# Graph experts and routed gated experts of the last layer in one block, the norm between them tile by tile, the gates in column groups

## The chip, the cores and the metric

The kernel runs on one core of one Trainium2 chip. Its engines are TensorE (PE, with its weight loads as PEld), VectorE (DVE), ScalarE (ACT), GpSimd (POOL) and SyncE (SP), each with its own queue of instructions; they wait for one another through semaphores. The metric is device time in microseconds (us), the median of several runs.

## What is computed

Four layers, each a graph layer and a feed-forward layer, on 512 tokens of 512 numbers. The change touches the feed-forward layer of layer 0 (only its gate) and both halves of layer 3:

```
# layer 3, graph half: 4 experts of two convolutions, the best 2 per token
gates = softmax(x @ gate_W + gate_b);  top_v, top_i = top_k(gates, 2)
sage_conv(h) = (sum of h over incoming edges / degree) @ W_l + b_l + h @ W_r
for e in 4 experts: h = x; for l in 2: h = relu(sage_conv(h))
out = sum over the chosen two of h_e * top_v
# layer 3, feed-forward half: 8 gated experts, the best 2 per token
logits = flat @ router_w.T;  topk_w = softmax(top_k(logits, 2))
y = (silu(flat @ w_gate) * (flat @ w_up)) @ w_down,   summed with topk_w
# around both
x = x + graph(_layernorm(x));   x = x + ffn(_layernorm(x))
```

Layer 0's feed-forward half routes each token to the best of 8 experts.

## The kernel before

Tokens are held as T = 4 tiles of P = 128 rows: `k.X` is the running sum, `k.N` its normed rows, `k.NT` the same turned (features on the partitions). PSUM has 8 banks, `k.ps[:, b, :]`. The program is written engine by engine; within an engine the written order is the order of work, and there is no scheduler. A `nc.Block()` holds one stage for all engines, and ends when all have ended it.

- **Gate** (`Routing`). `products` multiplies the gate's weights (8 or 4 columns) with `NT`, four matmuls that accumulate in 8 or 4 partitions (L829). ACT copies the result to SBUF (L892), `turns` (L836) turns it to rows of tokens, and `vector` (from L854 or L857) picks the experts. It is used in layer 0's feed-forward half and twice in layer 3.
- **Norm** (`Norm`). DVE makes statistics of all four tiles (L519, L522), ACT one root (L546), DVE the rows (L526), PE 16 transposes (L557), ACT and DVE two copies each (L549, L540). Ahead of its first wait PE runs 9 matmuls on zeros (`keep_busy`, L292).
- **Routed experts** (`RoutedFfn`). After the gate PE counts ranks (L1053, L1056) from the chosen experts' marks. DVE works out each token's place in a list sorted by expert, in granules of 128. The first granule is gathered by PE with a one-hot matrix (`place`, L1178; L1065), all others go by way of memory: POOL scatters all rows to `spread_d` (L1311, 8 indirect transfers of 128 rows in layer 3, 4 in layer 0), and when all have landed SP loads the second granule's tokens (L1023) and weights. PE then multiplies granule by granule: first weights (L1088), turn of the next granule's tokens (L1070), second weights (L1107). SP issues, ahead of all this, the gate's weights (L821), zeros for `spread_d` (L961) and the first granule's weights (L972, L977).
- **Graph experts** (`sage`). For each of 4 experts PE runs: own and neighbour products of layer 1 (L2888, L2920), two products of layer 2 for all four tiles (L2931, then L2936), and then the neighbour sums for all four tiles (L2943), which need the first product cut into a high and a low part (`hi`, `lo`: L2994, L2995; semaphore `ready`). DVE adds tile by tile into X (L2999, L3003 to L3007). Experts 0 and 1 are written out, 2 and 3 run in a loop. Weights lie in two sets `W[0]`, `W[1]`; SP loads expert e's when expert e - 2 has ended (`heads`).

Layer 3's graph half is one block, its feed-forward half the next; the second starts with `Norm`.

## Time and profile before

| what | value |
|---|---|
| time, median of 3 runs | 2035.28 us (2035.04 to 2037.95) |
| the profiled execution, whole / span of the trace | 2033.54 / 2031.8 us |
| PE busy | 1898.8 us, 93% |
| DVE / ACT / POOL busy | 952.7 / 499.7 / 318.8 us |
| mean TensorE clock granted | 0.974 of full speed |
| stages that the change touches | layer 0 gate 318 to 334, graph experts 1508 to 1781, last norm, gate and experts 1781 to 2032 us |

All times within the trace count from the span's start. A row of the timeline gives start, duration, engine, line, operation, what is written and read, shape, count, and in brackets how long the engine was idle before and who ended that. An f32 matmul is recorded as two instructions, a transpose as one. Busy time of PE says little by itself, since matmuls overlap; the distance between the starts of rows says what they cost.

### The profile page before, as it was taken

What the parts mean: (1) busy time and instruction counts of PE and PEld (TensorE: products, weight loads), DVE (VectorE), ACT (ScalarE), POOL (GpSimd) and SP (SyncE); (2) the same over time, 40 slices, a digit from 0 to 9 for tenths busy, and PEclk for the clock granted to TensorE, in tenths of its full rate; (3) what the DMA queues carried; (4) which work ended last, traced back from release to release, by engine and by line L of the source; (5) the groups of instructions that cost most, each with busy time, mean ns of one, the idle gap of its engine ahead of it and who ended that gap; (6) DMA issues with size and microseconds to landing.
All of it is one profiled execution on the core that took longest, in us unless ns stands there. A gap on an engine that the chain in (4) does not pass through costs nothing. (4 is left out here: it accounts for less than half of the span.)

```text
span 2031.8 us, 27351 instructions
## 1 busy us (share of the span) xinstructions
PE 1898.8 (93%) x8967; PEld 1042.6 (51%) x8967; DVE 952.7 (47%) x2888; ACT 499.7 (25%) x1379; POOL 318.8 (16%) x342
## 2 busy tenths in 40 slices
PE   8998997999989999999999799879789999979999
PEld 4454455766735434543453333334434444458876
DVE  7464455100069886998698721156432223240102
ACT  0153352111134361225224412137110000010000
POOL 0000000333407502740471000000000000010001
PEclk9999998999989999999999899989899999989999
DMA  4003008998358603740578199943352220089884
GB/s 165 1 1 104 1 2 333 399 358 328 118 170 268 179 1 129 238 119 1 150 214 284 41 329 386 386 144 127 124 180 80 88 88 0 0 311 403 326 316 157
DMA packets 180666, 358.02 MB, mean 176 GB/s; under 512 B 28816, under 2 KB 38304, under 8 KB 180524
## 3 DMA queue, kind: packets, MB, share of 16 engines
q1 hardware_dynamic: 157548, 285.94, 38.9%
q0 software_dynamic: 22976, 70.23, 11.6%
q8 instruction: 84, 1.38, 0.3%
q14 instruction: 58, 0.48, 0.1%
HBM read 334.43 MB, written 21.69 MB: 175 GB/s over the span
## 5 line engine op out<-in xcount | busy, mean ns | idle before, releaser
L1088 PEld LDWEIGHTS ps<-tokT,w 128*128 128x128 f32 x2304 | 259.8, 192 | 10.7 <-issue 6.7
L1088 PE MATMUL ps<-tokT,w 128*128 128x128 f32 x2304 | 260.6, 275 | 3.1 <-DVE tokT L1233 3.1
L1546 POOL DMA_INDIRECT w<-xl_d,src_i x216 | 213.3, 987 | 293.3 <-DMA xl_d<-XL 225.2
L1642 PE MATMUL ps<-XP,wide 128*128 (+1 forms) x456 | 185.2, 507 | 0.0
L1647 PE MATMUL ps<-w,ident 128*128 128x512 f32 x270 | 140.3, 601 | 8.2 <-DMA w<-xl_d,src_i 7.9
L1642 PEld LDWEIGHTS ps<-XP,wide 128*128 128x128 f32 x456 | 81.6, 189 | 72.6 <-issue 67.3
L1757 ACT ACTIVATE wide<-oht 128x128 fp32r<-128x128 bf16 x228 | 68.1, 308 | 196.9 <-PE ps L1647 176.9
L1311 POOL DMA_INDIRECT spread_d<-N,slot x12 | 11.8, 980 | 664.3 <-DVE slot L1192 661.2
L1107 PE MATMUL ps<-w,O 128*128 128x512 f32 x256 | 111.2, 592 | 0.0
L1919 DVE SCALAR_TENSOR_TENSOR w<-ps,w 128x512 f32<-128x512 f32 x144 | 98.1, 682 | 4.1 <-PE ps L1647 3.7
L1247 DVE TENSOR_TENSOR hT<-act,ps 128x512 f32<-128x512 f32 x20 | 13.8, 688 | 178.5 <-ACT act L1140 178.5
L1942 DVE SCALAR_TENSOR_TENSOR M<-pen,L,M 128x128 bf16 (+1 forms) x228 | 78.8, 346 | 9.9 <-DVE L L1931 6.1
L1148 ACT ACTIVATE O<-ps,b 128x128 f32<-128x128 f32 x128 | 36.5, 368 | 188.4 <-PE ps L1088 188.4
L1107 PEld LDWEIGHTS ps<-w,O 128*128 128x128 f32 x256 | 48.0, 190 | 57.4 <-issue 57.4
L261 POOL DMA_INDIRECT edges_d<-payload,slots x68 | 65.3, 960 | 49.2 <-ACT O L1148 35.7
L1689 PE MATMUL ps<-w 128*128 128x512 f16 x304 | 69.8, 380 | 1.6 <-DVE w L2002 1.0
L1107 PE MATMUL ps<-w,hT 128*128 128x512 f32 x160 | 70.3, 592 | 0.0
L392 PE MATMUL ps<-oh_d,oh_s 128*128 128x512 bf16 x272 | 67.3, 383 | 2.3 <-DVE oh_d L363 2.3
L292 PE MATMUL ps<-zero 128*128 128x512 bf16 x167 | 47.3, 439 | 22.4 <-PEq L2050 9.0
L2994 DVE CAST hi<-ps 128x512 fp32r<-128x512 f32 x16 | 11.1, 692 | 121.2 <-PE ps L2931 121.2
L2814 POOL DMA_INDIRECT tok<-rows_d,at_c x4 | 4.0, 1001 | 384.2 <-DVE at_c L2762 383.3
L1647 PEld LDWEIGHTS ps<-w,ident 128*128 128x128 f32 x270 | 48.4, 188 | 27.6 <-DMA w<-xl_d,src_i 18.2
(518 smaller groups left out, 3051.4 us busy)
## 6 DMA issues: line engine op xcount, KB each, us to landing
w<-L_ffn_W SPq DMA_DIRECT2D x16, 2048.0 KB, 12.8
w<-L_ffn_W SPq DMA_DIRECT2D x8, 4096.0 KB, 17.6
w<-fc1T SPq DMA_DIRECT2D x32, 1024.0 KB, 14.2
w<-fc2T SPq DMA_DIRECT2D x30, 1024.0 KB, 14.2
w<-L_ffn_w_gate SPq DMA_DIRECT2D x20, 1024.0 KB, 9.2
w<-L_ffn_w_up SPq DMA_DIRECT2D x20, 1024.0 KB, 12.1
w<-L_ffn_w_down SPq DMA_DIRECT2D x10, 2048.0 KB, 15.2
w<-L_ffn_w SPq DMA_DIRECT2D x8, 2048.0 KB, 13.2
```

The costliest lines, as they stand in the source:

```text
L261: gp.indirect_dma_start(k.edges_d, bass.IndirectOffsetOnAxis(ap=self.slot[:, j:j + 1].bitcast(U32), axis=0), self.pay[:, j, :], None).then ...
L292: m = pe.matmul(k.ps[:, b, :], k.zero16[:, 0:P], k.zero16[:], start=True, stop=True)
L392: pe.matmul(k.ps[:, T + t, :], oh_s[u][:, t * P:(t + 1) * P], oh_d[u][:], start=(i == 0), stop=(i == ET - 1))
L1088: m = pe.matmul(k.ps[:, 1 + (q * ins + i) % 4, s * P:(s + 1) * P], self.W1[u][i][:, f, (q * T + s) * P:(q * T + s + 1) * P], self.tokT[:, ...
L1107: m = pe.matmul(k.ps[:, 5 + u, :], self.hT[:, s, :], self.W2[u][:, s, :], start=(s == 0), stop=(s == self.HT - 1))
L1546: gp.indirect_dma_start(self.G[:, u, :], None, k.xl_d, bass.IndirectOffsetOnAxis(ap=k.src_i[:, i:i + 1].bitcast(U32), axis=0)).then_inc(k. ...
L1642: m = pe.matmul(bank, self.wide[:, i % DEEP, :], self.XP[:, q].rearrange("p t n -> p (t n)")[:, bass.ds(at, D)], start=False, stop=(q == 1 ...
L1647: m = pe.matmul(bank, k.ident[:], self.source(i), start=False, stop=True)
L1689: m = pe.matmul(k.ps[:, T:2 * T, :].rearrange("p b n -> p (b n)")[:, bass.ds(at, N)], half[u], self.os[l][u], start=False, stop=True, skip ...
L1757: a.activation(self.wide[:, i % DEEP, :], self.oht[:, i * P:(i + 1) * P], ACT.Copy).then_inc(self.widened.sem, 1)
L1919: v.scalar_tensor_tensor(self.r[i % QUAD], rows, 0.0, self.att8, ALU.max, ALU.mult, accum_out=self.sdot[:, i:i + 1]).then_inc(self.dotted. ...
L1942: v.scalar_tensor_tensor(low, self.pen[:, i * P:(i + 1) * P], self.L[:, i:i + 1], low, ALU.subtract, ALU.min).then_inc(self.low.sem, 1)
```

## The change

1. `Routing.products` writes each of its four matmuls to a group of 32 output partitions of its own (weights padded with zeros to 32 columns, `pad`, on POOL) and doesn't accumulate. `turns` becomes four matmuls with `k.pile`, a matrix that adds the four groups up while it turns them; `k.pile` is made once by one DVE reduction at the start of the program.
2. `RoutedFfn.tensor` gets 9 matmuls on zeros ahead of the ranks and 7 behind them, in both routed layers.
3. `sage` and the last `RoutedFfn` are one block. The experts' loop is written out. The experts' weights, some temporaries and the gate's rows lie in the routed layer's buffers: `W[0]` in its first granule's first weights.
4. SP issues the router's weights, the zeros and the first granule's second weights behind the last graph expert's weights, and the first granule's first weights as soon as graph expert 2 has ended.
5. PE runs L2936's product and the neighbour sum of a tile one after the other, for every expert, and DVE follows.
6. In the last expert the norm is made tile by tile (`TileNorm`), between the experts' tiles; the router's logits are made as rows of tokens (`row_logits`, moving side 8 columns), so that no turn is needed. 12 matmuls on zeros stand ahead of the last tile's transposes.

```diff
@@ Routing @@
     def products(self, pe, bank=0):
...
         for f in range(T):
-            m = pe.matmul(k.ps[0:width, bank, :], self.g[:, f, :], self.cols[:, f, :], start=(f == 0), stop=(f == T - 1))
+            m = pe.matmul(k.ps[f * GATE:(f + 1) * GATE, bank, :], self.g[:, f, :], self.cols[:, f, :],
+                          start=True, stop=True)
...
     def turns(self, pe, bank=0):
...
         for t in range(T):
-            m = pe.transpose(k.ps[:, bank, t * 8:t * 8 + width], self.logits_at[0:width, t * P:(t + 1) * P],
-                             k.ident[0:width, 0:width])
+            m = pe.matmul(k.ps[:, bank, t * 8:t * 8 + width], self.logits_at[:, t * P:(t + 1) * P],
+                          k.pile[:, 0:width], start=True, stop=True)
...
+    def row_logits(self, pe, t, bank):
...
+        for f in range(T):
+            m = pe.matmul(k.ps[:, bank, t * 8:t * 8 + width], self.cols[:, f, t * P:(t + 1) * P],
+                          self.g[:, f, 0:width], start=(f == 0), stop=(f == T - 1))
...
+class TileNorm:
...
+    def statistics(self, v, ch, t):
+        ch.link(v.bn_stats(self.st[:, t, :], self.x[:, t, :]))
+        v.bn_aggr(self.mv[:, t, :], self.st[:, t, :]).then_inc(self.stats.sem, 1)
+
+    def roots(self, a, t):
+        a.wait_ge(self.stats.sem, self.stats.at(t + 1))
+        a.activation(self.rstd[:, t:t + 1], self.mv[:, t, 1:2], ACT.Sqrt, bias=self.k.eps[:, 0:1]
+                     ).then_inc(self.root.sem, 1)
+
+    def normal(self, v, ch, t):
+        v.wait_ge(self.root.sem, self.root.at(t + 1))
+        ch.link(v.reciprocal(self.rstd[:, t:t + 1], self.rstd[:, t:t + 1]))
+        v.tensor_scalar(self.rows[:, t, :], self.x[:, t, :], self.mv[:, t, 0:1], self.rstd[:, t:t + 1],
+                        ALU.subtract, ALU.mult).then_inc(self.normed.sem, 1)
+
+    def turn(self, pe, t, bank):
+        pe.wait_ge(self.normed.sem, self.normed.at(t + 1))
+        for f in range(T):
+            m = pe.transpose(self.k.ps[:, bank, f * P:(f + 1) * P], self.rows[:, t, f * P:(f + 1) * P],
+                             self.k.ident[:])
+        m.then_inc(self.turned.sem, 1)
...
@@ RoutedFfn.tensor @@
+        keep_busy(pe, k, 3, 9)
         pe.wait_ge(k.chosen.sem, k.chosen.at(1))
...
         i.then_inc(k.ranks.sem, 1)
+        keep_busy(pe, k, 3, 7)
...
@@ sage, SP @@
                 for e in range(2, E):
                     sp.wait_ge(k.heads.sem, k.heads.at(e - 1))
                     weights(sp, e, e % 2)
+                ffn.r.sync(sp)
+                ffn.empty(sp)
+                ffn.second_weights(sp, 0, 0)
+                sp.wait_ge(k.heads.sem, k.heads.at(E - 1))
+                ffn.first_weights(sp, 0, 0)
+                ffn.sync(sp)
...
@@ sage, PE @@
                         m.then_inc(k.av.sem, 1)
-                    pe.wait_ge(k.ready.sem, k.ready.at(1) + e)
-                    for t in range(T):
+                        if e == E - 1 and t >= 2:
+                            closing.wait_columns(pe, t - 2)
+                            ffn.r.row_logits(pe, t - 2, 0)
+                        if t == 0:
+                            pe.wait_ge(k.ready.sem, k.ready.at(1 + e))
                         for part in (hi, lo):
...
                         m.then_inc(k.out.sem, 1)
-                walk(pe, step)
+                        if e == E - 1 and t:
+                            closing.turn(pe, t - 1, t - 1)
+                for e in range(E):
+                    step(e)
+                closing.wait_columns(pe, T - 2)
+                ffn.r.row_logits(pe, T - 2, 0)
+                keep_busy(pe, k, 5, 12)
+                closing.turn(pe, T - 1, T - 1)
+                closing.wait_columns(pe, T - 1)
+                ffn.r.row_logits(pe, T - 1, 0)
+                ffn.tensor(pe)
...
@@ sage, DVE, last expert @@
                         m = v.tensor_tensor(k.X[:, t, :], k.X[:, t, :], o[:, t, :], ALU.add)
-                    m.then_inc(k.heads.sem, 1)
-                    v.wait_ge(k.heads.sem, k.heads.at(1) + e)
+                        if e == E - 1:
+                            ch.link(m)
+                            closing.statistics(v, ch, t)
+                            closing.normal(v, ch, t)
```

PE's queue from the last graph expert's products of layer 2 to the last layer's ranks, before (in the loop's body, so the rows stand for experts 2 and 3):

```order
L2936 MATMUL ps<-w,H_347 128x512 x16
L2943 MATMUL ps<-hi,C 128x512 x4
L2943 MATMUL ps<-lo,C 128x512 x4
...
L2943 MATMUL ps<-hi,C 128x512 x4
L2943 MATMUL ps<-lo,C 128x512 x4
...
L292 MATMUL ps<-zero_20 128x512 x9
L557 MATMUL ps<-ident,N 128x128 x16
L829 MATMUL ps<-NT,gate 8x512 x4
L836 MATMUL ps<-ident,tok 128x8 x4
L1053 MATMUL ps<-m,beforeb 128x8
```

The same place after, from the last expert's third tile on (L3030 is the product that was L2936, L3040 the neighbour sum, L959 the transposes, L907 the gate rows, L293 the matmuls on zeros, L1130 the ranks):

```order
L3030 MATMUL ps<-w_358,H_396 128x512 x4
L907 MATMUL ps<-gate,NT 128x8 x4
...
L959 MATMUL ps<-ident,N 128x128 x4
L3030 MATMUL ps<-w_358,H_396 128x512 x4
L907 MATMUL ps<-gate,NT 128x8 x4
...
L959 MATMUL ps<-ident,N 128x128 x4
L907 MATMUL ps<-gate,NT 128x8 x4
L293 MATMUL ps<-zero_20 128x512 x12
L959 MATMUL ps<-ident,N 128x128 x4
L907 MATMUL ps<-gate,NT 128x8 x4
L293 MATMUL ps<-zero_20 128x512 x9
L1130 MATMUL ps<-m,beforeb 128x8
```

What moved: products, sums, transposes and gate rows of different tiles now alternate (where "..." stands after, the sum of that tile is left out, two rows of L3040), and only one tile's transposes and gate rows are left behind the last sum.

SP's queue at the same place, before (the last rows of the graph block, then the next block):

```order
L2849 DMA b_362<-sage_b 128x512
L2861 UNCONDITIONAL_BRANCH
...
L821 DMA gate<-router_wT 128x4x8
L961 DMA spread_d<-zrow 128x512 x14
L972 DMA w_381<-L_ffn_w_gate 128x4x512
L972 DMA w_382<-L_ffn_w_up 128x4x512
...
L977 DMA w_385<-L_ffn_w_down 128x8x512
```

And after:

```order
L2937 DMA b_403<-sage_b 128x512
L827 DMA gate<-router_wT 128x4x8
L1038 DMA spread_d<-zrow 128x512 x14
L1052 DMA w_359<-L_ffn_w_down 128x8x512
L1047 DMA w_355<-L_ffn_w_gate 128x4x512 [waits heads]
L1047 DMA w_356<-L_ffn_w_up 128x4x512
```

What moved: no block border stands between the graph weights and the routed layer's, the second weights come ahead of the first, and the first wait for graph expert 2 alone.

## Rows read from the trace of the kernel before

**Rows 1.** The page, first part: busy us, share of the span, instructions.

```profile
PE 1898.8 (93%) x8967; PEld 1042.6 (51%) x8967; DVE 952.7 (47%) x2888; ACT 499.7 (25%) x1379; POOL 318.8 (16%) x342
```

**Rows 2.** Timeline, last graph expert, PE and DVE.

```profile
1757.43 13.90 PE L2936 MATMUL ps<-w,H 128*128 128x512 f32 x32
...
1758.36 0.69 DVE L2995 TENSOR_TENSOR lo<-ps,hi 128x512 fp32r<-128x512 f32 x1
...
1773.04 1.09 PE L2943 MATMUL ps<-hi,C 128*128 128x512 f32 x4
1773.30 0.75 DVE L3003 SCALAR_TENSOR_TENSOR o<-ps,inv_deg,o 128x512 f32<-128x512 f32 x1 [1.24 <-PE ps L2943]
...
1774.90 1.09 PE L2943 MATMUL ps<-hi,C 128*128 128x512 f32 x4
...
1780.35 0.69 DVE L3007 TENSOR_TENSOR X<-X,o 128x512 f32<-128x512 f32 x1
```

**Rows 3.** Timeline, from the last norm to the second granule.

```profile
1781.57 3.72 PE L292 MATMUL ps<-zero 128*128 128x512 bf16 x9 [2.78 <-PEq L2861]
1781.57 2.47 DVE L519 BATCH_NORM_STATS2 stats<-X 128x6 f32<-128x512 f32 x4 [0.53 <-PEq L2861]
...
1784.49 0.30 ACT L546 ACTIVATE rstd<-mv,eps 128x4 f32<-128x4 f32 x1 [1.67 <-DVE mv L522]
...
1785.63 2.03 PE L557 MATMUL ps<-ident,N 128*128 128x128 f32 x16 [0.34 <-DVE N L526]
1787.37 1.08 ACT L549 ACTIVATE NT<-ps 128x512 f32<-128x512 f32 x2 [2.58 <-PE ps L557]
...
1788.83 3.60 PE L829 MATMUL ps<-NT,gate 128*8 128x512 f32 x8 [1.16 <-DVE NT L540]
...
1793.55 0.19 DVE L857 COPY lg<-ps 128x32 f32<-128x32 f32 x1 [4.78 <-PE ps L836]
...
1795.65 0.19 PE L1053 MATMUL ps<-m,beforeb 128*128 128x8 bf16 x1 [2.14 <-DVE m L1168]
...
1797.68 6.06 PE L1065 MATMUL ps<-w,N 128*128 128x128 f32 x32 [1.49 <-DVE w L1178]
...
1804.53 14.56 PE L1088 MATMUL ps<-tokT,w 128*128 128x128 f32 x128 [0.78 <-DVE tokT L1233]
...
1820.16 0.66 PE L1070 MATMUL ps<-ident,tok 128*128 128x128 f32 x4 [1.08 <-DMA tok<-spread_d]
```

**Rows 4.** The same timeline, last scatter on POOL, then SP.

```profile
1809.22 0.96 POOL L1311 DMA_INDIRECT spread_d<-N,slot  x1 [0.30 <-issue]
...
1817.67 0.34 SPq L1023 DMA_DIRECT2D tok<-spread_d  x1
```

**Rows 5.** Timeline, gate of layer 0, PE alone.

```profile
322.39 0.41 PE L836 MATMUL ps<-ident,tok 8*128 8x8 f32 x4 [0.68 <-ACT tok L892]
326.33 0.19 PE L1053 MATMUL ps<-m,beforeb 128*128 128x8 bf16 x1 [3.54 <-DVE m L1166]
...
328.11 5.31 PE L1065 MATMUL ps<-w,N 128*128 128x128 f32 x32 [1.24 <-DVE w L1178]
334.21 1.05 PE L1088 MATMUL ps<-tokT,w 128*128 128x128 f32 x7 [0.79 <-DVE tokT L1233]
```

**Rows 6.** Stretches: length, busy us by engine, granted clock, DMA share, GB/s.

```profile
325.00:330.00 5.00, 2.42 (x23) 2.34 (x24) 3.93 (x27) 0.17 (x1) 0.00 (x0) 0.50 1.04 388
...
1796.00:1802.00 6.00, 4.51 (x28) 4.42 (x25) 4.25 (x24) 1.21 (x1) 1.38 (x2) 0.50 1.05 409
```

**Rows 7.** Groups by form, PE: busy us, mean ns of one, idle before.

```profile
L2690 PE MATMUL ps<-w,hT 128*32 128x512 f32 x64 | 7.7, 598 | 3.2 <-ACT hT L2806 3.2
...
L2706 PE MATMUL ps<-g,NT 128*128 128x16 f32 x32 | 4.8, 298 | 1.2 <-PEq L449 1.2
```

**Rows 8.** DMA issues of two stretches: count, median us from issue to landing.

```profile
spread_d<-N,slot POOLq DMA_INDIRECT x8, 6.5
...
NT<-result_d,back_slot POOLq DMA_INDIRECT x4, 3.5
```

More of the change, by code:

```diff
@@ L50 @@
 EX_SCALE = 16384.0
+GATE = P // T
 class Ticker:
@@ new lines, with __init__, columns, wait_columns @@
+class TileNorm:
+    def __init__(self, k, c, x, rows, cols):
+        self.k, self.x, self.rows, self.cols = k, x, rows, cols
+        self.stats, self.root, self.normed, self.turned, self.cols_out = signals(
+            c, k, "tile_stats", "tile_root", "tile_rows", "tile_turned", "tile_columns")
+        self.st, self.mv, self.rstd = sb(c, k, "stats", [P, T, 6]), sb(c, k, "mv", [P, T, 2]), sb(c, k, "rstd", [P, T])
+    def statistics(self, v, ch, t):
[16 more added lines that the diff above has]
+        m.then_inc(self.turned.sem, 1)
+    def columns(self, a, t, bank):
+        a.wait_ge(self.turned.sem, self.turned.at(t + 1))
+        a.activation(self.cols[:, :, t * P:(t + 1) * P],
+                     self.k.ps[:, bank, :].rearrange("p (f n) -> p f n", f=T), ACT.Copy).then_inc(self.cols_out.sem, 1)
+    def wait_columns(self, eng, t):
+        eng.wait_ge(self.cols_out.sem, self.cols_out.at(t + 1))
@@ L899, in done, with __init__ @@
     def done(self):
-        k = self.k
-        done((k.gate_loaded, 32 if self.bias is not None else 16), (k.gate_mm, 1), (k.gate_rows, 1), (k.gate_turned, 1), (k.gate_ready, 1), (k.gate_exped, 1))
+        done((self.stats, T), (self.root, T), (self.normed, T), (self.turned, T), (self.cols_out, T))
 class RoutedFfn:
-    def __init__(self, k, c, r, norm, granules, w, hidden, gated, spread, result, beside=None, spare=None, y=None):
+    def __init__(self, k, c, r, norm, granules, w, hidden, gated, spread, result, beside=None, spare=None, y=None,
+                 joined=False):
@@ L912, in __init__ @@
         self.k, self.r, self.norm, self.granules, self.w, self.gated, self.beside = k, r, norm, granules, w, gated, beside
-        self.rows, self.out = norm.rows, y
+        self.rows, self.out, self.joined = norm.rows, y, joined
         self.summed, self.last_placed, self.last_turned, self.last_cols, self.last_added = signals(
@@ L1046, in tensor @@
         n_first, n_second, n_third = self.counts()
-        self.norm.tensor(pe)
-        self.norm.wait_cols(pe)
-        self.r.tensor(pe)
+        if not self.joined:
+            self.norm.tensor(pe)
+            self.norm.wait_cols(pe)
+            self.r.tensor(pe)
+        keep_busy(pe, k, 3, 9)
         pe.wait_ge(k.chosen.sem, k.chosen.at(1))
@@ L1126, in scalar @@
         k, quads, ins = self.k, self.quads, self.ins
-        self.norm.scalar(a)
-        self.r.scalar(a)
+        if self.joined:
+            self.r.exps(a)
+        else:
+            self.norm.scalar(a)
+            self.r.scalar(a)
         signal = k.ffn_act if self.gated else k.ffn_hidden
@@ L1223, in vector @@
         k, quads = self.k, self.quads
-        self.norm.vector(v)
+        if not self.joined:
+            self.norm.vector(v)
         self.r.vector(v, chosen=self.choose)
@@ L1306, in pool @@
         k, choices, G = self.k, self.r.choices, self.granules
+        if not self.joined:
+            self.r.pad(gp)
         gp.wait_ge(k.emptied.sem, k.emptied.at(16 * (G - 1)))
@@ L2861, in sage @@
         with nc.Block() as block:
-            def walk(eng, step):
-                for u in range(2):
-                    step(u, u, 0)
-                with eng.Fori(1, E // 2) as j:
-                    for u in range(2):
-                        step(j * 2 + u, u, j)
             @block.sync
@@ L2902, in means, with step @@
                         m.then_inc(neighbors.sem, 1)
-                def step(e, u, j):
-                    if not later(e, 1):
+                def step(e):
+                    u = e % 2
+                    if e == 0:
                         pe.wait_ge(rooted.sem, rooted.at(16))
```

153 lines of the change are left out of this document (95 added, 58 removed).

## The prediction, before the changed kernel ran

> **What bounds the kernel now.** I read the page first: TensorE (PE) is busy for 93% of the span [rows 1], so whatever shortens the time must either take work off PE or close one of its pauses. The chain that ended last does not reach back far enough to help, so I went through the timeline of the three places that the diff touches, and asked at each who waits last.
>
> The last expert of the graph layer [rows 2] is a PE stretch without pause: the fourth product of each tile (L2936) for all four tiles, 13.90 us, that is 3.43 a tile, and then the neighbour sums (L2943), 1.87 us a tile (1773.04 to 1774.90). VectorE (DVE) follows them at 1.9 us a tile and ends its last addition to X at 1781.04. Then [rows 3] comes a chain in which every engine works on all four tiles and hands them on whole: statistics 1781.57, root 1784.49, transposes 1785.63, gate product 1788.83, routing from 1793.55, ranks 1795.65, the first granule's gather 1797.68, and only at 1804.53 the first expert product. From the end of PE's last neighbour sum (1773.04 + 3 x 1.87 = 1778.64) to there it is 25.9 us, in which PE does little that counts. The first product of the second granule waits again, 1.08 us, for rows that were scattered to memory and read back: the scatters were issued from 1800.32 to 1809.22 and the row tile asked for at 1817.67 [rows 4]. After that PE has no pause worth naming, so what is gained up to there is kept. The gate of the first routed layer has the same shape [rows 5]: turn 322.39, ranks 326.33 after 3.54 us of pause, gather 328.11.
>
> TensorE's granted clock was 0.50 in both stretches in which ranks and gather stand [rows 6], the lower of its two levels (1.2 GHz); before each, PE had been mostly idle while DVE chose experts.
>
> **The change, part by part.**
>
> Gate in column groups (first routed layer and graph layer). Four matmuls of 8 or 4 output partitions that accumulated now go to four groups of 32 output partitions. Before: 3.60 us for 8 recorded instructions (two for each f32 matmul) [rows 3, 7]. Nearest row: L2690, also 32 partitions by 512 elements in four groups, 64 in 7.7 us, so 0.12 each and about 1.0 for the 8. Saved: 2.6. From both sides: nothing, if the groups didn't run together (3.6), and 2.7. L2690 has the very shape, so I take 2.6. The turn becomes four f32 matmuls with a full 128x128 stationary side: 8 instructions. L2706 with 16 columns took 0.15 each, partly at the lower clock [rows 7], L1088 0.114 each at the higher one (14.56 over 128) [rows 3]. I take 0.12, 1.0 in all against 0.41, so 0.6 lost (bounds 0.5 and 0.8). Net 2.0 in each layer. In the graph layer nothing else waits there: weights and inverse degrees are there early. The Trainium skill ("TensorE: Matmul & The Clock Gate", Part 3, measured speedup) gives 2.38 times for three column tiles; by that rule four would give, as an estimate, about 3 and save 2.4 instead of 2.6, where this trace shows 3.6 (0.43 over 0.12).
>
> Fill matmuls in both routed layers: 9 ahead of the ranks, 7 behind them. Nine of them took 3.72 at the lower clock [rows 3], so about 1.9 at the higher and 1.5 for seven. The pause ahead of the ranks is 3.54 in the first layer [rows 5] and 2.14 in the last [rows 3]: the nine are covered at the higher clock, and not at the lower (3.7). The seven fill a pause of 1.24 [rows 5] and 1.49 [rows 3]: 0.3 and 0.1 lost. What they give: if the clock stays up, the gather of 32 instructions costs 32 x 0.114 plus a tail, 3.8, in place of 5.31 and 6.06: 1.5 and 2.3 gained. First layer in sum: -2.0 + 0.3 - 1.5 = **-3.2**. Its first weights were there when the tokens' copy was (PE went on 0.79 after it [rows 5]); the queue is full until past 330 [rows 6], so if they had landed only then, up to 3.2 would go: the low bound of this term is 0. Graph layer: **-2.0**.
>
> Loops written out, output sums between products (all experts). PE now does product and sum tile by tile; the same instructions in another order, so 0 as long as the first sum finds its high and low parts ready. They are ready at 1759.05 (1758.36 and 0.69) and would be wanted at 1757.43 + 3.43 = 1760.86 [rows 2]: 1.8 us in hand. Weights for the last routed layer's first granule and the zeros move ahead into the last two experts, where the queue has nothing to carry.
>
> Last norm tile by tile. PE does four more things before the last tile's sum ends: transposes of tiles 0 and 1 (2.03 / 4 = 0.5 each [rows 3]) and their gate rows (8 x 0.12 = 0.95 each): +2.9, so 1778.64 becomes 1781.5, and X of tile 3, 2.25 later as now (0.26, then 1.99), 1783.75. From there, for one tile, by [rows 3]: statistics 2.47 / 4 = 0.62, from their end to the root at most 0.45 (1784.04 to 1784.49), the root 0.30, from its end to the first transpose 0.84 (1784.79 to 1785.63): 2.2, so the rows are there at 1786.0. PE meanwhile: transposes of tile 2 (0.5), its copy (0.2 and 0.54), its gate rows (0.95), then 12 fill matmuls (12 x 0.21 = 2.6): free at 1786.4. The fill is the last to end, by 0.4. Then transposes 0.7 with tail, copy 0.65, gate rows 1.1: DVE reads the logits at 1788.9, against 1793.55: **-4.65**. The new exponential's table load falls into the routing, as now. With gather (-2.3) and fill (+0.1) the first expert product starts 6.85 earlier, at 1797.7, and ends at 1812.25.
>
> Second granule. Its rows hang on the scatter, which only moves by 4.65: last issue 1804.57. The issue costs the same on GpSimd (POOL). But before, weights kept the DMA engines full (share 1.05 [rows 6]): a scatter took 6.5 us to land, an indirect transfer with a quiet queue 3.5 [rows 8]. After, the weights are there already. From the last issue to SP's request it was 8.45 [rows 4]; with 3.5 in place of 6.5 it is 5.45 (bounds 3.5 and 8.45): asked for at 1810.0, there 2.5 after that (1817.67 to 1820.16 now): 1812.5. PE comes at 1812.25 and waits 0.25. Last layer in sum, by the second granule's start: 1812.5 - 1820.16 = **-7.7**.
>
> Constants: one small reduction on DVE at the start, +0.2 (0 if hidden).
>
> Sum: -3.2 - 2.0 - 7.7 + 0.2 = -12.7. The profiled execution took 2033.54, the median of the three runs is 2035.28, so I set the change against the median: **2022.6 us**.
>
> **Rivals.**
> 1. Clock. In the first layer the turn would end at 320.8 (322.39 - 2.6 + 1.0), the nine at 322.7, and the ranks start at 324.3 (326.33 - 2.0): PE still idles for 1.6 us. If the clock falls there as it does now, seven fillers cost 2.9 for a pause of 1.24 (+1.65) and the gather stays at 5.3: the layer gives 0.35 instead of 3.2, total 2025.4. For it: rows of 0.50 after pauses; against: the pause is less than half of the old one. Chance 0.20.
> 2. The same in the last layer: nine fillers 3.7 against a cover of 2.1 (+1.7), seven +1.5, gather 6.8 (+3.0). The layer gives 1.7 instead of 7.7 (1820.16 against 1812.25 + 6.2), total 2028.6, and 2031.4 with rival 1 as well. The Trainium skill has a rule for this ("TensorE: Matmul & The Clock Gate", Part 4): transposes don't count as activity for the clock. Against it, between the transposes stand 12 + 9 + 7 real matmuls and no pause above 0.9. Chance alone 0.05, both 0.05.
> 3. The scatter lands no sooner with a quiet queue. Then 1804.57 + 8.45 + 2.5 = 1815.5, PE waits 3.2, total 2025.6. Against it speaks [rows 8]. Chance 0.08.
> 4. Slower: PE now meets the wait for high and low parts after one tile's product and not after four. Were DVE late by x beyond the 1.8 in hand, each of four experts would cost x. To end slower than before by 0.2% it takes 17 us, 4.2 an expert, so DVE ready 6 us later than in [rows 2]. DVE is idle for over 2 us between its pairs of casts. Chance 0.03.
> 5. The column groups don't overlap: 5.2 lost, total 2027.8. Chance 0.04.
>
> **How the numbers follow.** All works as summed: 0.50, between 2018.5 and 2024.5 (copy and handoff times, the 12 fillers, drift of the clock elsewhere). With rivals 1 to 5 at 0.45 and 0.05 for what I don't see. 2018 to 2029 leaves out both clocks low, the slower case and half of the unseen on either side, 0.12 or so. A measurement of this kernel can tell about 0.2%, 4 us, from no change. Faster by more than that: 0.50 + 0.20 + 0.05 + 0.08 + 0.04 and some of the unseen, 0.89; within 0.2%: both clocks low and some of the unseen, 0.07; slower: 0.04.
>
> **What the profile of the changed kernel would show.** The gate product at about 1.0 us; granted clock 1.00 from the ranks through the gather in both layers and a gather under 4 us; DVE's logits copy some 7.4 us after the last neighbour sum's end; W1 of the last layer 16 us after it and not 25.9; scatters that land in under 4 us and no PE pause before the second granule; PE without pauses in the four experts. A PE pause ahead of the first neighbour sum, or a clock of 0.50 at the gather, or more than 1 us waiting for the scattered rows, would make it wrong.

## The result, and the profile after

The changed kernel took 2017.3 us (median of 4 runs, 2016.1 to 2019.47) against 2035.16 us for the kernel before (4 runs beside it, 2032.65 to 2037.95). The ratio is 0.9913, with a 95% interval of 0.9896 to 0.993, so it is faster, by 0.9%. The forecast was 2022.6 in a range from 2018 to 2029: the sign and most of the mechanism hold (in layer 0 the clock did not do what was forecast), and the time lies 0.7 us below the range.

The page of the kernel after, first part (busy us, share of the span, instructions), answers to [rows 1]. PE is busy for 4.1 us less, although 44 matmuls on zeros were added (the nine of the last norm, L292, are gone), and the span is 14.2 us shorter: the other 10.1 us are pauses that are closed or filled, and PE's share of the span goes from 93% to 94%.

```profile
span 2017.6 us, 27480 instructions
PE 1894.7 (94%) x9030; PEld 1044.4 (52%) x9030; DVE 953.2 (47%) x2890; ACT 500.6 (25%) x1383; POOL 318.9 (16%) x344
```

**The last layer.** Timeline of the kernel after, from the last expert to the second granule (start, length, engine, line, operation, count, idle before and what ended it). It answers to [rows 2 to 4].

```profile
1751.86 3.60 PE L3030 MATMUL ps<-w,H 128*128 128x512 f32 x8
...
1775.71 0.60 PE L959 MATMUL ps<-ident,N 128*128 128x128 f32 x4
...
1776.99 1.06 PE L907 MATMUL ps<-gate,NT 128*128 128x8 f32 x8 [0.69 <-ACT NT L965]
...
1777.91 2.75 PE L293 MATMUL ps<-zero 128*128 128x512 bf16 x12
...
1779.48 0.55 DVE L953 TENSOR_SCALAR N<-X,mv,rstd 128x512 f32<-128x512 f32 x1
...
1780.49 0.60 PE L959 MATMUL ps<-ident,N 128*128 128x128 f32 x4
...
1781.78 1.06 PE L907 MATMUL ps<-gate,NT 128*128 128x8 f32 x8 [0.69 <-ACT NT L965]
...
1782.69 2.10 PE L293 MATMUL ps<-zero 128*128 128x512 bf16 x9
1782.88 0.19 DVE L869 COPY lg<-ps 128x32 f32<-128x32 f32 x1 [2.85 <-PE ps L907]
...
1784.98 0.18 PE L1130 MATMUL ps<-m,beforeb 128*128 128x8 bf16 x1 [0.19 <-DVE m L1249]
...
1787.01 3.84 PE L1143 MATMUL ps<-w,N 128*128 128x128 f32 x32
...
1791.63 14.56 PE L1166 MATMUL ps<-tokT,w 128*128 128x128 f32 x128 [0.78 <-DVE tokT L1315]
...
1798.58 0.96 POOL L1395 DMA_INDIRECT spread_d<-N,slot  x1 [0.30 <-issue]
...
1802.13 0.34 SPq L1098 DMA_DIRECT2D tok<-spread_d  x1
...
1806.03 0.60 PE L1148 MATMUL ps<-ident,tok 128*128 128x128 f32 x4
```

Count everything from the last expert's fourth product (L3030; L2936 in [rows 2]). To the logits copy it is now 31.02 us (1782.88 - 1751.86), before 36.12 (1793.55 - 1757.43): -5.10. From the copy to the ranks (2.10) and on to the gather (2.03) nothing has changed, so the fill matmuls cost nothing there. From the gather to the first expert product 4.62 in place of 6.85: -2.23. From there to the second granule 14.40 in place of 15.63: -1.23, most of it the pause of 1.08 for the scattered rows, which is gone. In all -8.56.

Its stretches (length, busy us by engine, granted clock, DMA share, GB/s), which answer to the second row of [rows 6]:

```profile
1516.00:1700.00 184.00, 184.00 (x487) 91.43 (x486) 50.12 (x100) 10.26 (x16) 0.00 (x0) 1.00 0.31 111
1700.00:1800.00 100.00, 97.66 (x391) 56.45 (x389) 36.49 (x95) 10.97 (x17) 7.75 (x8) 1.00 0.17 61
1800.00:2017.00 217.00, 212.07 (x1416) 170.65 (x1414) 31.51 (x57) 17.32 (x29) 12.66 (x17) 1.00 0.82 300
```

The granted clock stays at its higher level (2.4 GHz) through the ranks and the gather. The DMA issues from 1785 to 1805 (count, KB each, median us to landing), beside [rows 8]:

```profile
tok<-spread_d SPq DMA_DIRECT2D x1, 256.0 KB, 2.6
spread_d<-N,slot POOLq DMA_INDIRECT x8, 2.9
```

**The gate of layer 0.** The same kernel's timeline, PE alone, beside [rows 5]:

```profile
320.20 1.93 PE L840 MATMUL ps<-NT,gate 128*32 128x512 f32 x8 [0.95 <-DVE NT L543]
322.85 1.88 PE L848 MATMUL ps<-pile,tok 128*128 128x8 f32 x8 [0.72 <-ACT tok L915]
324.58 3.60 PE L293 MATMUL ps<-zero 128*128 128x512 bf16 x9
328.13 0.18 PE L1130 MATMUL ps<-m,beforeb 128*128 128x8 bf16 x1
...
328.49 1.67 PE L293 MATMUL ps<-zero 128*128 128x512 bf16 x7
330.00 3.73 PE L1143 MATMUL ps<-w,N 128*128 128x128 f32 x32
334.52 5.74 PE L1166 MATMUL ps<-tokT,w 128*128 128x128 f32 x49 [0.78 <-DVE tokT L1315]
```

Product, turn and the nine fill matmuls ran at the lower clock (1.2 GHz): 1.93 and 1.88 in place of the 1.0 that was forecast for each, and the nine took 3.60. The clock came back while they ran, and PE had no pause ahead of the ranks. Nor did the nine hold the ranks up. They start at 328.13, 0.06 us after DVE has made the marks that they read, as they do where PE stands waiting for these (old gate, below):

```profile
327.89 0.18 DVE L1247 CAST m<-masks 128x32 bf16<-128x32 f32 x1
```

The gather took 3.73, at the higher clock. From the gate product to the first expert product: 14.3 us.

**The gate of the graph layer**, the same view:

```profile
1513.22 1.06 PE L840 MATMUL ps<-NT,gate 128*32 128x512 f32 x8 [0.99 <-DVE NT L543]
...
1518.65 0.95 PE L848 MATMUL ps<-pile,tok 128*128 128x4 f32 x8
...
1537.31 4.88 PE L3014 MATMUL ps<-A,w 128*128 128x512 f32 x11
```

Both as forecast; from the gate product to the first product with the neighbour means (L3014) 24.09 us, 26.26 in the kernel before.

### The profile page after: what moved, and what is told of

Its sections match the earlier page's. It is cut to its first block and busy times, and to the rows that moved or that the text cites. A ratio compares the mean times of both kernels' runs of the same rounds, so it can differ in the third digit from the quotient of the medians.

```text
span 2017.6 us, 27480 instructions
## 1 busy us (share of the span) xinstructions
PE 1894.7 (94%) x9030; PEld 1044.4 (52%) x9030; DVE 953.2 (47%) x2890; ACT 500.6 (25%) x1383; POOL 318.9 (16%) x344
## 5 line engine op out<-in xcount | busy, mean ns | idle before, releaser
L293 PE MATMUL ps<-zero 128*128 128x512 bf16 x202 | 51.8, 407 | 19.9 <-PEq L2137 9.0
L2325 PE MATMUL ps<-w,xa 128*64 128x512 f32 x256 | 58.1, 597 | 3.9 <-issue 2.9
## 6 DMA issues: line engine op xcount, KB each, us to landing
w<-fc1T SPq DMA_DIRECT2D x32, 1024.0 KB, 14.2
w<-fc2T SPq DMA_DIRECT2D x30, 1024.0 KB, 14.2
w<-L_ffn_w_up SPq DMA_DIRECT2D x20, 1024.0 KB, 12.7
```

The costliest lines, as they stand in the source:

```text
L2325: m = pe.matmul(k.ps[u * SL:(u + 1) * SL, q, :], XA[:, f, e * SL:(e + 1) * SL], W1[u][:, f, q * 512:(q + 1) * 512], start=(f == 0), stop=( ...
```

## The experiments

Each kernel was timed beside the kernel before on the same chip. Chips and executions differ by more than some of the effects (the kernel before had medians from 2033.6 to 2035.4), so runs are compared by their ratio to the kernel before; 0.001 is 2.0 us. Each ratio has an interval of some 0.0012 to 0.0024 either way, 2 to 5 us. What is finer than that is read from the stretches of the profiles, which stand together in the table at the end of this section. Every kernel computes all of the output.

**The two kernels again**, unedited, for the spread.

> The changed kernel once more, against the kernel before. The trace of the changed kernel shows 12.9 us less in the three places that the change touches (first gate 2.0, graph layer's gate 2.2, last layer 8.7), while the medians differ by 17.9. Theory A (the places are all of it, the rest is drift of untouched stages from run to run): with more rounds the difference falls to 12 to 15 us, 2020 to 2023 where before is 2035, and the untouched stages move by other amounts in this profile than in the first. Theory B (something outside the three places became shorter for good): the difference stays at 16 to 20 us, and the same untouched stages are shorter by the same amounts again.

> The kernel before, unchanged, against itself: what a comparison tells from nothing. Both theories: within 1.5 us of the kernel before. In its profile, theory A expects the starts of untouched stages (the second attention, the graph attention, the positional layer) to differ from the first profile of the same kernel by 1 to 3 us, as they do between before and after; theory B expects less than 1 us.

Measured: after 2017.51 (6 runs, 2014.37 to 2021.99), ratio 0.9911 (0.9895 to 0.9928). Before 2033.58 (12 runs, 2029.39 to 2038.27), ratio to its own other runs 0.9994 (0.9982 to 1.0006). So the gain is there again: 17.9 us against the medians beside it, as theory B has it, and 16.1 against these 12 runs. But nothing outside the three places became shorter for good: what is left of the span without them was 1926.7 and 1924.0 in the kernel before, 1925.0 and 1925.7 in the kernel after, and that is theory A. Timeline of the second profile of the kernel before, layer 0, and two of its stretches:

```profile
318.36 5.61 PE L829 MATMUL ps<-NT,gate 128*8 128x512 f32 x8 [0.95 <-DVE NT L540]
...
330.34 6.57 PE L1065 MATMUL ps<-w,N 128*128 128x128 f32 x32 [1.24 <-DVE w L1178]
337.69 2.50 PE L1088 MATMUL ps<-tokT,w 128*128 128x128 f32 x20 [0.78 <-DVE tokT L1233]
```

```profile
316.00:320.00 4.00, 3.04 (x9) 1.23 (x8) 1.29 (x2) 1.08 (x2) 0.00 (x0) 0.50 1.02 414
...
332.00:336.00 4.00, 4.00 (x20) 4.00 (x20) 1.11 (x7) 0.00 (x0) 2.47 (x3) 0.50 1.05 385
```

The same code, 3.2 us longer than in [rows 5] (19.3 from gate product to first expert product against 16.1): this time the low clock lay over the gate product (5.61) and over the whole gather (6.57 against 5.31). The forecast had priced the first layer from one execution, in which the low clock fell beside the work.

**All fill matmuls taken out.**

```diff
-        keep_busy(pe, k, 3, 9)
...
-        keep_busy(pe, k, 3, 7)
...
-                keep_busy(pe, k, 5, 12)
```

> The changed kernel without its matmuls on zeros (9 and 7 in both routed layers, 12 ahead of the last tile). If they are what keeps the clock up in the last layer, ranks and gather there run at a granted 0.50 again and the gather takes about 6 us and not 3.8: slower than the changed kernel by some 2 to 3 us there; in the first layer, where nine of them ran at the lower clock, next to nothing changes for the nine, and the gather is longer by 1 to 1.5. In all 3 to 4.5 us slower than the changed kernel. Rival (the fillers only cost PE time, the clock stays up by itself since the chain got shorter): 1 us faster than the changed kernel, gather 3.8 in the last layer.

Measured: 2024.72, ratio 0.9947 (0.9929 to 0.9964), so some 7 us of the gain hang on them by the ratios, more than the 3 to 4.5 expected. Its timeline at the two gathers:

```profile
328.05 5.81 PE L1141 MATMUL ps<-w,N 128*128 128x128 f32 x32 [1.24 <-DVE w L1257]
```

```profile
1791.25 6.35 PE L1141 MATMUL ps<-w,N 128*128 128x128 f32 x32 [1.49 <-DVE w L1257]
```

Its stretches say +2.0 in layer 0 and +3.4 in the last, 5.4 together. The rival, that the clock stays up by itself, falls.

**The fill matmuls put into the kernel before** (nine ahead of the ranks, seven behind, nothing else).

```diff
         self.r.tensor(pe)
+        clear_banks(pe, k, [3] * 9)
         pe.wait_ge(k.chosen.sem, k.chosen.at(1))
...
         i.then_inc(k.ranks.sem, 1)
+        clear_banks(pe, k, [3] * 7)
```

> The kernel before with nothing but the matmuls on zeros, 9 ahead of the ranks and 7 behind them, in both routed layers. Theory C (the gate of layer 0 is longer or shorter by where the clock happens to be low, 16.1 and 19.3 us from gate product to first expert product in two profiles of before, and fillers hold it at its shortest): about 15 us there in this profile, and 1 to 4 us off the whole, 2031 to 2034. In the last layer the gather takes 3.8, but the second granule's start stays 41.7 us behind the last neighbour sum, since it hangs on the scatter. Rival D (the fillers are worth 7 us wherever they stand, as the median without them says): 2027 to 2029.

Measured: 2030.94 (12 runs), ratio 0.9991 (0.9975 to 1.0007): no gain that this can tell. In its profile both gathers are short (3.73 and 3.84), and layer 0 gains 1.5 us (14.61, about the 15 that theory C names). The last layer's expert product starts 2.2 us earlier (44.88 us after the fourth product, not 47.10), but from there to the second granule it takes 16.99 in place of 15.63, because the scattered rows are late on the full queue, and behind that pause of 2.43 the clock falls once more (+1.7). In the last layer, alone, the fill matmuls run into the next wait. Rival D (7 us wherever they stand) falls.

**Only the 12 taken out, and 6 left of the 12.**

```diff
-                keep_busy(pe, k, 5, 12)
```

```diff
-                keep_busy(pe, k, 5, 12)
+                keep_busy(pe, k, 5, 6)
```

> The kernel after without the 12 fill matmuls between the last but one tile's gate rows and the last tile's transposes; the 9 and 7 around the ranks stay. Theory A, the nine and seven alone hold the clock: the last tile's transposes start 0.4 us earlier, as its rows were ready then, and the time is 2017.1. Theory B, TensorE's idle 2.3 us there are enough for the granted clock to be 0.50 at the ranks: the nine take 3.6, the seven 2.9 and the gather 6.1 in place of 1.8, 1.7 and 3.8, and the second granule starts some 3.5 us later: 2021.

> The kernel after with 6 fill matmuls in place of the 12. Theory A, six hold the clock as well and end before the last tile's rows are ready: the second granule starts 0.4 us earlier, 2017.1. Theory B, half of them is too little and the granted clock falls to 0.50 at the ranks: 2021.

Measured: 2017.67, ratio 0.9923 (0.9903 to 0.9942), and 2017.2, 0.9918 (0.99 to 0.9937). Neither can be told from the kernel after. The timeline without the 12, and its stretches:

```profile
1777.00 1.12 PE L959 MATMUL ps<-ident,N 128*128 128x128 f32 x4 [2.03 <-DVE N L953]
1778.80 1.88 PE L907 MATMUL ps<-gate,NT 128*128 128x8 f32 x8 [0.69 <-ACT NT L965]
1780.91 3.06 PE L293 MATMUL ps<-zero 128*128 128x512 bf16 x8 [0.23 <-issue]
...
1785.67 3.73 PE L1143 MATMUL ps<-w,N 128*128 128x128 f32 x32
```

```profile
1776.00:1780.00 4.00, 2.31 (x10) 1.92 (x10) 0.71 (x2) 2.00 (x3) 0.00 (x0) 0.56 0.00 0
1780.00:1784.00 4.00, 3.77 (x20) 1.93 (x21) 2.47 (x21) 1.16 (x3) 0.00 (x0) 0.59 0.00 0
1784.00:1788.00 4.00, 4.00 (x40) 3.20 (x38) 3.21 (x18) 0.38 (x1) 0.00 (x0) 1.00 0.00 0
```

Neither theory was right. The clock did fall, as B said, beside a pause of 2.03 and PE's transposes, and the transposes and gate rows cost double. But it rose while the nine behind them ran, and the gather ran at the higher clock. The nine held the ranks up here, by 1.0 us (3.09 from the logits copy to the ranks in place of 2.10). The price by the profile is 1.6 us (six: 0.7), not 3.5.

**The gate as it was**, in both layers that have it: accumulated product and transposes.

```diff
-            m = pe.matmul(k.ps[f * GATE:(f + 1) * GATE, bank, :], self.g[:, f, :], self.cols[:, f, :],
-                          start=True, stop=True)
+            m = pe.matmul(k.ps[0:width, bank, :], self.g[:, f, 0:width], self.cols[:, f, :],
+                          start=(f == 0), stop=(f == T - 1))
...
-            m = pe.matmul(k.ps[:, bank, t * 8:t * 8 + width], self.logits_at[:, t * P:(t + 1) * P],
-                          k.pile[:, 0:width], start=True, stop=True)
+            m = pe.transpose(k.ps[:, bank, t * 8:t * 8 + width], self.logits_at[0:width, t * P:(t + 1) * P],
+                             k.ident[0:width, 0:width])
...
```

> The changed kernel with the gate's products as one accumulation in 8 or 4 partitions and the transposes, as before. Both theories: 2.2 us more from the graph layer's gate product to its first neighbour product (26.3 against 24.1). In layer 0 theory C expects 1 to 2 us more, since fillers still keep the clock up. In all 3 to 4 us slower than the changed kernel. If column groups were worth more than that in the whole, 2023 or above, they would do something outside their own place.

Measured: 2020.32, ratio 0.9932 (0.9909 to 0.9955), which alone can't be told from the kernel after. The graph layer's stretch is back at 26.27 (+2.2). Layer 0 costs only 0.3 more (14.61 against 14.31), less than the 1 to 2 expected, but these two are not alike: in this execution product and turn ran at the higher clock, in the kernel after at the lower one. In two of the kernels below that keep the new gate (weights late, order of sums) they ran at the higher clock too, and the stretch is 12.7 there. Like with like, the column groups give 1.9 in layer 0.

**The last norm on all four tiles**, behind the last expert (the tile-wise statistics, roots, copies, transposes and gate rows out of the last expert, and the 12 with them).

```diff
-                        if e == E - 1 and t >= 2:
-                            closing.wait_columns(pe, t - 2)
-                            ffn.r.row_logits(pe, t - 2, 0)
...
-        ffn = RoutedFfn(k, c, r3, TileNorm(k, c, k.X, k.N, k.NT), G3,
+        ffn = RoutedFfn(k, c, r3, Norm(k, c, k.X, k.N, k.NT), G3,
...
```

> The changed kernel with the last norm on all four tiles after the last expert, and the gate by products and turn, as in the other layers; joined block, weights ahead, column groups and the 9 and 7 fillers stay. The sum from rows: logits some 2 us earlier than before (column groups), gather 3.8 and not 6.1, scatter onto an empty queue, and PE spared the 2.6 us of transposes and gate rows between its sums. Second granule 36.3 us behind the last neighbour sum, where the changed kernel has 30.6 and its last sum 2.6 later: 3 us slower than the changed kernel, about 2020.5. If tile by tile is most of the gain (5 us or more), the sum misses something in the norm.

Measured: 2020.51, ratio 0.9936 (0.9912 to 0.996), which alone can't be told from the kernel after either. From the last expert's fourth product to the second granule 59.24 us, 5.1 more than in the kernel after. Timeline, PE:

```profile
1778.68 3.67 PE L560 MATMUL ps<-ident,N 128*128 128x128 f32 x16 [0.83 <-DVE N L529]
...
1786.25 3.53 PE L293 MATMUL ps<-zero 128*128 128x512 bf16 x9
...
1791.48 3.73 PE L1143 MATMUL ps<-w,N 128*128 128x128 f32 x32
```

The clock fell again: the transposes of the whole norm (3.67 in place of the 2.03 of [rows 3]) and most of the nine (3.53) ran at the lower one. From the first transpose to the gate product it is 4.63 us, 3.20 in the kernel before, and from the logits copy to the ranks 3.18 in place of 2.10, since the nine end late. Those are 2.5 us; what is left of the 5.1 is near the 3 us that were expected for the chain of four tiles.

**Weights and zeros late**: the last routed layer's first weights and the zeros are issued only behind the last tile's statistics.

```diff
                 ffn.r.sync(sp)
-                ffn.empty(sp)
-                ffn.second_weights(sp, 0, 0)
                 sp.wait_ge(k.heads.sem, k.heads.at(E - 1))
+                sp.wait_ge(closing.stats.sem, closing.stats.at(T))
+                ffn.empty(sp)
                 ffn.first_weights(sp, 0, 0)
+                ffn.second_weights(sp, 0, 0)
```

> The changed kernel with zeros, first and second weights of the first granule issued only when the last tile's statistics are there, as late as before relative to the norm. If the weights have to be ahead for the shorter chain to count: PE waits for the first weights until about 1798, 6.5 us after the tokens are turned, and the scatter waits for the zeros: 5 to 7 us slower than the changed kernel, 2023 to 2025. Rival (PE would not have waited, the weights' place is worth only the scatter's landing): 0 to 2 us slower.

Measured: 2025.3 (12 runs), ratio 0.9959 (0.9944 to 0.9974). Timeline, PE, and its DMA issues:

```profile
1793.09 9.73 PE L1166 MATMUL ps<-tokT,w 128*128 128x128 f32 x64 [6.87 <-DMA w<-L_ffn_w_up]
1803.82 7.41 PE L1166 MATMUL ps<-tokT,w 128*128 128x128 f32 x64 [1.01 <-DMA w<-L_ffn_w_up]
```

```profile
w<-L_ffn_w_up SPq DMA_DIRECT2D x2, 1024.0 KB, 13.9
...
spread_d<-N,slot POOLq DMA_INDIRECT x8, 7.0
```

The second granule starts 9.7 us later, more than the 5 to 7 expected: 6.1 of them are there at the first expert product, and 3.6 come behind it, since its first 64 instructions ran partly at the lower clock behind the long pause (9.73, against 7.41 for the next 64) and PE waited once more (1.01). A faster chain needs its weights sooner, so moving them ahead is not free cover: without it the other parts lose more than half of their gain. The scatters took 7.0 beside these loads; here that cost nothing, since PE came later still.

**The queue kept full while the scatters run**: three more loads of 1 MB into dead tiles, their data unused, and the second weights behind them.

```diff
-                ffn.second_weights(sp, 0, 0)
                 sp.wait_ge(k.heads.sem, k.heads.at(E - 1))
                 ffn.first_weights(sp, 0, 0)
+                sp.wait_ge(k.chosen.sem, k.chosen.at(1))
+                for n, m in enumerate((A0, H1, o)):
+                    sp.dma_start(m[:], ...).then_inc(k.loaded.sem, 16)
+                ffn.second_weights(sp, 0, 0)
                 ffn.sync(sp)
+                sp.wait_ge(k.loaded.sem, k.loaded.at(48))
```

> The changed kernel with the first granule's second weights (2 MB) and 3 MB of loads that nobody reads issued when the experts are chosen, so that the DMA queues are full while the tokens are scattered, as they were before. If the full queue made the scatter slow: landing 6 to 7 us after each issue instead of 2.7 to 3.8, SP asks for the tokens some 3 us later, PE waits 1.5 to 3 us ahead of the second granule, and the kernel is 1.5 to 3 us slower than the changed one. Rival (the scatter's landing has its own length): no pause, and the same time.

Measured: 2017.73 (4 runs, 2015.91 to 2024.43), ratio 0.9911 (0.9893 to 0.9929): not to be told from the kernel after. Its profile (of the execution that took 2024.43) shows the mechanism, in the DMA issues, the timeline and one stretch:

```profile
spread_d<-N,slot POOLq DMA_INDIRECT x8, 7.0
```

```profile
1809.30 0.66 PE L1148 MATMUL ps<-ident,tok 128*128 128x128 f32 x4 [2.54 <-DMA tok<-spread_d]
1809.79 8.73 PE L1185 MATMUL ps<-w,hT 128*128 128x512 f32 x16
```

```profile
1812.00:1816.00 4.00, 4.00 (x9) 1.82 (x8) 0.50 (x1) 0.00 (x0) 0.00 (x0) 0.82 1.05 396
```

A scatter took 7.0 us to land in place of 2.9, and PE waited 2.54. Behind the pause the clock fell, and the sixteen products took 8.73 in place of 7.03 (in the kernel before they took 7.03 behind a pause of 1.08). The stretches say +2.7 to the second granule and +1.7 behind it. The median doesn't show these 4.4 us, and the record doesn't say why: the other three runs took 2015.91 to 2018.58, and only the slowest of the four was profiled. So the mechanism is shown in one execution, and its price in the time is not.

**The order of sums and products**: experts 0 to 2 with all products first, as before.

```diff
+                        if e < E - 1:
+                            continue
...
+                    if e < E - 1:
+                        pe.wait_ge(k.ready.sem, k.ready.at(1 + e))
+                        for t in range(T):
+                            for part in (hi, lo):
...
```

> The kernel after with the neighbour sums of experts 0 to 2 behind all four products of the expert, as before; the last expert is as after. Theory A, the order is worth nothing: from the first neighbour product to the last expert's fourth product 214.6 us as in both kernels, 2017.5. Theory B, a part of the gain that the stretches of single profiles don't show comes from this order (DVE's and ScalarE's work beside it is spread otherwise): 2019 to 2020.

Measured: 2018.11, ratio 0.993 (0.9907 to 0.9952), no difference that can be told; its three stretches are those of the kernel after or shorter. The stretch that the order touches, from L3014 to the last expert's fourth product, settles it: 214.63 us here, 214.55 in the kernel after, 214.65 in the kernel before. The order is worth nothing: theory A.

**Three parts undone at once**: fills out, old gate, norm on all tiles (the edits above together).

> The kernel after with three things undone at once: the accumulated gate product and its transposes are back, the fill matmuls (9, 7 and 12) are gone, and the last norm works on all tiles after the last expert. Left of the change are the zeros around the ranks, the weights of the last routed layer ahead, and the neighbour sums tile by tile between the products. Undone one at a time, the three cost 2.8, 7.2 and 3.0 us. Theory A, the three add up and the rest is worth nothing but what they had in common: 2017.5 + 13 = 2030.5, and by the two stretches of a single profile (gate to first expert product of the first layer 16 to 19 us, last neighbour sum to second granule about 41.8 us) as before. Theory B, they share a cost (the low clock at the gather is counted in both the fills and the norm): less, about 2027. Theory C, they hide each other's cost and nothing else of the change gains: the time of before, 2034 to 2035.

Measured: 2034.06 (12 runs), ratio 0.9997 (0.9982 to 1.0012): the time of the kernel before, so what is left in this kernel (weights and zeros ahead, tile-wise order, one block) gives nothing by itself that can be told. That is theory C's time. But theory C also says that the three hide each other's cost, and they don't: by ratios to the kernel before, the three (fills, gate, norm) cost 3.5, 2.0 and 2.4 thousandths singly, 7.9 together, and 8.5 at once, that is 16 and 17 us: within the intervals they add up, as theory A has it. (The medians of different chips, laid beside each other without the ratio, would say 13 and 16.6.) The same three in the profiles: 5.4, 2.5 and 5.1 singly, 13.0 together, and 12.9 at once.

**All stretches.** Worked out from the traces, in us: A from layer 0's gate product to its first expert product, B from the graph layer's gate product to L3014, C from the last expert's fourth product to the second granule; "rest" is the span without the three.

```
                 A       B       C      rest     span
before         16.10   26.26   62.73  1926.7   2031.8
before again   19.34   26.26   62.68  1924.0   2032.3
undo three     16.22   26.26   62.99  1924.6   2030.0
before + fill  14.61   26.26   61.87  1924.9   2027.6
no fill        16.30   24.09   57.58  1926.4   2024.3
after          14.31   24.09   54.16  1925.0   2017.6
after again    14.32   24.09   54.16  1925.7   2018.3
old gate       14.61   26.27   54.15  1927.9   2023.0
whole norm     15.36   24.09   59.24  1923.3   2022.0
late weights   12.68   24.07   63.85  1922.1   2022.6
busy queue     14.31   24.08   56.88  1927.4   2022.6
no twelve      14.31   24.08   55.79  1922.0   2016.2
six of twelve  14.31   24.07   54.86  1926.7   2019.9
sums last      12.70   24.09   54.16  1925.1   2016.0
```

B repeats to 0.02 us and C to 0.3 within a form of the kernel. A depends on where the low clock falls. The rest, which no edit touches, moves by 6 us from one execution to the next, with no leaning to either side. Before and before again against after and after again: A -3.4, B -2.2, C -8.5, together -14.1, and the spans say -14.1 too.

## Why the forecast was right in kind and too narrow in size

**The gate in column groups, -2.0 in each layer.** The graph layer gave -2.2: product 1.06 in place of 3.60 [rows 3], turn 0.95, both as costed. Rival 5 (no overlap) falls. The old gate put back 2.2 there. In layer 0 product and turn took 1.93 and 1.88 at the lower clock; only where they ran at the higher one do the groups give the 2.0 there too (1.9, old gate against weights late and order of sums).

**Fill matmuls and clock in layer 0, -3.2 in sum.** This term failed. It was priced from one profile, 16.10, and against that profile the layer gave 1.8 (14.31). That two profiles against two give 3.4 is luck: the second profile of the kernel before has 19.34. Forecast was a clock that stays up; in fact product, turn and nine ran at the lower one, in six of the eight kernels that have column groups and fills (14.31 to 15.36). In the other two, product and turn ran at the higher one, and the stretch is 12.7, near the 12.9 that the forecast asks for. What the forecast feared in rival 1 (the low clock ahead of the ranks) did happen in the kernel after. Its price did not follow: the nine took 3.6 and filled a pause that is 3.40 us without them (fills out), so that they did not hold up the ranks, the seven took 1.67, not 2.9, and the gather was at the higher clock. The four profiles without the nine have it at 5.31 to 6.57, the ten with them at 3.73. The low bound of this term (weights landing late) was no matter.

**Last norm tile by tile, logits at -4.65.** -5.10: PE's additions before the last sum's end were 2.6 (forecast 2.9), and from there to the copy 7.2 (forecast 7.4). As forecast, the 12 were the last to end: N was ready at 1780.03 and PE free for it at 1780.49. What they give is the clock at the transposes and behind them, 1.6 us net by the profile, which the forecast didn't ask about. Rival 2 falls: the granted clock is 1.00 in every stretch from 1516 to the end. On its rule in the Trainium skill ("TensorE: Matmul & The Clock Gate", Part 4, transposes are no activity for the clock) these runs are in keeping and no proof: with real matmuls between the transposes the clock stayed up, without the 12 it fell beside a pause and transposes.

**Gather -2.3, fill +0.1.** -2.23 and 0.

**Second granule at -7.7.** -8.56. The scatter's landing was forecast at 3.5 us on a quiet queue, from [rows 8]; it took 2.9, and SP's request came 3.55 after the last issue in place of the 5.45 costed, so PE came last and had no pause (0.25 forecast). Rival 3 falls; the busy queue showed its price, 7.0 to land and 2.5 of pause.

**Order of sums, 0.** As forecast; rival 4 falls, no PE pause in the four experts. **Weights ahead** were costed at nothing, hidden in an idle queue. Undone, they cost 9.7: without them the shortened chain meets the landing of the first weights. **Constants, +0.2:** one DVE reduction of 0.197 us; whether it is hidden no run shows.

**The step that failed** is in "How the numbers follow": "All works as summed: 0.50, between 2018.5 and 2024.5", and the low end of 2018 set from it. Two terms of the sum were mis-sized: the last layer, 8.5 against 7.7 (the scatter's landing and the 0.45 in the logits), and layer 0, 1.8 against 3.2 by the profile it was priced from, 3.4 with the second one. In all the profiled executions give 14.1 against 12.7, 1.4 us more. That would be 2021, inside the range. The remaining 3.8 us are between what the profiled executions show (-14.1) and what the medians show (-17.9 in both sets of runs). The forecast set its sum against a median of three runs and left no room on the low side for what executions differ by, although "rest" alone moves by 6 us and A by 3.2; against that, 4.6 us under the sum was too little, where it had left 6.4 above it for the rivals. Executions of one kernel spread further still: 2027.7 to 2040.04 before, 2014.37 to 2021.99 after.

**What stays open** is how much of those 3.8 us is real. 14.1 us would be a ratio of 0.9931, just above the upper ends of the two intervals (0.993 and 0.9928). A part is which executions were profiled: the two of the kernel after took 2019.47 and 2020.01, 2.2 and 2.5 above their medians, those of the kernel before 2033.54 and 2033.99, 1.7 below the median and 0.4 above it. All 73 runs of the kernel before have a mean of 2034.4, the 10 of the kernel after one of 2017.6, 16.8 less. The executions without a profile could have a costlier layer 0 in the kernel before (A has the room: 16.1 to 19.3 in three profiles), or it is chance. That undoing three parts brings back the whole 17 us by medians says that, if real, it is in these parts and not in the order or the early weights; the profile of that kernel shows only 13.

## What to carry to other kernels

Where PE waits for a chain of DVE work and then runs transposes or a gather, a few matmuls on zeros ahead of it had the clock up again when the work came: here 9 did, in both layers and in every profile that has them. They cost next to nothing where the wait was about as long as they (3.4 to 3.5 us in layer 0, even at the lower clock; 2.1 in the last layer, at the higher one). They held the ranks up by 1.0 to 1.2 us where it was not (the 2.1 of the last layer, at the lower clock: without the 12, with six of them, and with the norm on all tiles). Put alone into the last layer they ran into the next wait; the gain came with tile-wise handing on and with transfers issued where the queue is idle, and each part has to be costed in the presence of the others. Before a sum is set against a median, profile the kernel before twice: one stretch that depends on where the low clock falls differed by 3.2 us, as much as the whole term that was priced from it.

## What was not expected of the hardware

- Where the low clock falls is not a property of the code. In layer 0 it lay at the gate product and the gather in one execution of the kernel before (5.61 and 6.57) and beside the product, over part of the gather, in another (19.3 against 16.1 us for the same instructions).
- A pause of PE of 2.4 to 2.5 us ahead of the second granule (two profiles) was followed by a lower granted clock (0.75 and then 0.82 in the stretches of 4 us from its end in one, 0.79 and 0.78 in the other) and cost 1.7 more than the pause; one of 1.08 us at the same place (kernel before) did not.
- An indirect scatter (eight carried 2.10 MB) landed in 2.9 us on a quiet queue and in 7.0 beside weight loads, with the same scatter code; four column groups of f32 matmuls with 32 output partitions took 1.06 us for what took 3.60 one after the other, 3.4 times.
